# Turning the attended heads and their sums by VectorE block transposes in place of TensorE passes, in a four-layer gated cross-attention kernel

## What is computed

```python
query = _split_heads(q @ w_q.T + b_q)
key = _split_heads(k @ w_k.T + b_k)
value = _split_heads(v @ w_v.T + b_v)
scores = jnp.einsum('bhqd,bhkd->bhqk', query, key) / jnp.sqrt(jnp.asarray(D_K, query.dtype))
scores = jnp.where(mask == 0, jnp.asarray(-1000000000.0, scores.dtype), scores)
attn = jax.nn.softmax(scores, axis=-1)
out = jnp.einsum('bhqk,bhkd->bhqd', attn, value)
out = out.transpose(0, 2, 1, 3).reshape(B, -1, D_MODEL)
return out @ w_o.T + b_o
```

## Time and profile before

| | |
|---|---|
| median of 3 runs | 1608.25 us (1605.38 to 1609.08) |
| profiled execution, its own time | 1611.25 us |
| its span in the profile | 1609.4 us |
| PE busy | 1483.6 us, 92% |
| DVE busy | 1318.3 us, 82% |
| ACT busy | 1135.4 us, 71% |
| POOL busy | 1030.6 us, 64% |
| mean granted TensorE clock | 0.963 |

### The profile page before, as it was taken

One profiled execution on the slowest core, in us unless ns is written; L12 is line 12 of the kernel. 1 busy time (PEld: TensorE's weight loads), 2 busy tenths in 40 slices (PEclk: granted clock), 3 DMA queues, 4 the chain that ended last, 5 costly groups with the idle time before them and its releaser, 6 DMA issues.

```text
span 1609.4 us, 42630 instructions
## 1 busy us (share of the span) xinstructions
PE 1483.6 (92%) x14155; PEld 1141.0 (71%) x14155; DVE 1318.3 (82%) x3187; ACT 1135.4 (71%) x2057; POOL 1030.6 (64%) x1392
## 2 busy tenths in 40 slices
PE   3899999999999974478999999999999999999997
PEld 2788888888888863245676677777777777767666
DVE  4798888888888876787888889898988888898732
ACT  7798888888888743265666666676666666666664
POOL 4688888888888743324456565666656565665445
PEclk8899999999999995588999999999999999999999
DMA  6322322322322002422222232233322332233100
GB/s 225 107 73 67 96 67 65 97 65 74 89 65 72 1 1 85 139 83 72 78 81 75 83 88 79 79 87 85 87 81 78 84 86 78 82 83 86 56 17 21
DMA packets 197690, 125.45 MB, mean 78 GB/s; under 512 B 44400, under 2 KB 196848, under 8 KB 197360
## 3 DMA queue, kind: packets, MB, share of 16 engines
q1 hardware_dynamic: 197616, 124.48, 26.7%
HBM read 92.69 MB, written 25.17 MB: 73 GB/s over the span
## 4 chain that ended last, share of the span: by engine, by line
PE 46%; SPq 6%; DMA 3%; DVE 2%; issue 2%; POOL 1%; ACT 1%; POOLq 0%
PE b_bank L1837 27%; PE b_bank L1912 6%; PE b_scoreT L1894 4%; PE b_score L1877 4%; PE b_bank L1845 2%; SPq L1293 2%; DMA b_nmT<-b_nm 1%; SPq L1282 1%; PE b_bank L1989 1%; SPq L1309 1%; PE b_bank L1927 1%; DMA b_yT<-b_y 1%; SPq L1318 1%; DVE b_nm L1653 1%; SPq L1326 1%
## 5 line engine op out<-in xcount | busy, mean ns | idle before, releaser
L1471 ACT ACTIVATE b_E<-b_scoreT 128x1024 f32<-128x1024 f32 x256 | 262.2, 1024 | 151.4 <-PE b_scoreT L1894 151.1
L1653 DVE TENSOR_REDUCE b_nm<-b_score 128x4 bf16<-128x1024 f32 x256 | 313.3, 1224 | 57.4 <-PE b_score L1877 51.2
L31 ACT ACT_TABLE_LOAD x157 | 201.4, 1283 | 18.6 <-PEq L1059 15.2
L1837 PE MATMUL b_bank<-f,b_YT 128*128 128x256 bf16 x1536 | 193.0, 277 | 4.7 <-POOL b_YT L1404 4.6
L890 PE MATMUL bank<-hT,W1T 128*128 128x256 bf16 x1536 | 183.3, 273 | 2.4 <-DVE hT L706 1.6
L1837 PE MATMUL b_bank<-b_hT,f 128*128 128x256 bf16 x1536 | 183.4, 273 | 0.8 <-DVE X L1749 0.8
L890 PE MATMUL bank<-W2T,G 128*128 128x256 bf16 x1024 | 171.0, 272 | 6.7 <-DVE GT L780 6.2
L1837 PEld LDWEIGHTS b_bank<-f,b_YT 128*128 128x128 bf16 x1536 | 144.7, 99 | 40.8 <-issue 19.3
L1837 PEld LDWEIGHTS b_bank<-b_hT,f 128*128 128x128 bf16 x1536 | 147.7, 98 | 30.4 <-issue 12.6
L890 PEld LDWEIGHTS bank<-hT,W1T 128*128 128x128 bf16 x1536 | 147.9, 98 | 27.8 <-ACT G L549 4.1
L1388 POOL TENSOR_TENSOR b_v<-b_v,b_e 128x512 f32<-128x512 f32 x32 | 40.7, 1270 | 194.1 <-DVE b_e L1734 194.1
(11 more groups left out here) (222 smaller groups left out, 3537.1 us busy)
## 6 DMA issues: line engine op xcount, KB each, us to landing
b_Q<-q_dram SPq DMA_DIRECT2D x192, 64.0 KB, 2.5
b_K<-k_dram SPq DMA_DIRECT2D x192, 64.0 KB, 2.7
xin<-in_x SPq DMA_DIRECT2D x32, 256.0 KB, 3.1
ctxn<-in_ctx SPq DMA_DIRECT2D x32, 256.0 KB, 2.8
mask_in<-in_mask SPq DMA_DIRECT2D x32, 256.0 KB, 3.0
X<-in_x SPq DMA_DIRECT2D x32, 256.0 KB, 4.0
ctxt<-in_ctxT SPq DMA_DIRECT2D x32, 256.0 KB, 4.2
b_ctxt<-in_ctxT SPq DMA_DIRECT2D x32, 256.0 KB, 2.8
```

What stands on the lines that cost most here:

```text
L31: act.add_instruction(mybir.InstLoadActFuncSet(name=nc.get_next_instruction_name(), act_func_set_id=which, ins=[], outs=[]))
L1471: nc.scalar.activation(E[:, pair:pair + 2], scoreT_ps[:, :, :, :], ACT.Exp).then_inc(sig["E"], 1)
L1653: nc.vector.tensor_reduce(pair, score_ps[:, :, :, :], AX.X, ALU.max, negate=True).then_inc(sig["nm"], 1)
L1837: last = nc.tensor.matmul(out_tile, lhs(i, k), rhs(j, k), start=start and k == chunks[0] and (i, j) == TERMS[0], stop=stop and k == chunks ...
```

## The change

DVE's transpose turns each 32x32 block within its own place. With a head 32 rows high, one such instruction on a bank of 128x512 gives for each block of 32 tokens a square in which the tokens lie along the partitions, and the head's 16 values and its sum along the free axis. So the change makes the turn there, for all tokens together and straight from PSUM, and the turn back in the same way.

- ACT no longer has `heads_copy(0)` and `heads_copy(1)`.
- PE no longer has `heads_transposed(0)`, `(1)` and `attended_transposed`: 12 passes of 128x128 for each batch. The first part of `second_product` now stands ahead of the turn of `hn`.
- DVE gets `heads_turned(0)` behind `maxima(6)`, on batch a; `heads_turned(1)` behind `mlp_normalised`, on batch o; `inverse_sums` (one reciprocal of 32 elements on a partition) and `attended` (one product of 512) behind `scaled`; and `heads_back` (the turn back) behind `maxima(0)`. It loses two reciprocals of 16 and two products of 256.
- `attended_high` and `attended_low` read the result `oF` from SBUF, where they read a PSUM bank before.
- The order of features after the turn back differs from the one before; the output weights' rows and the values' bias are put in that order on the host (`by_heads`).
- Banks: OT0, OT1 and ON fall away. AV01 and AV23 now share bank 8 with hT, H1 goes to bank 9 with K and V, H3 to bank 7.

```diff
@@ TURNS
             7: [("xT", "xlo", L_QKV, 1, 1), ("Q", "qlo", L_QKV, 1, 1), ("FFN", "ob", L_FFN, 1, 1),
-                ("PROJ", "x3", L_PROJ, 1, 1), ("H0", "Y", L_MLP, 4, 1), ("V", "V", L_QKV, 1, 1)],
-            8: [("OT0", "on", L_PROJ, 2, 1), ("hT", "hlo", L_MLP, 1, 1), ("ON", "onlo", L_PROJ, 1, 1),
-                ("AV01", "oS", L_ATT, 2, 1), ("H1", "Y", L_MLP, 4, 2)],
-            9: [("OT1", "on", L_PROJ, 2, 2), ("K", "klo", L_QKV, 1, 1), ("AV23", "oS", L_ATT, 2, 2),
-                ("H3", "Y", L_MLP, 4, 4)],
+                ("PROJ", "x3", L_PROJ, 1, 1), ("H0", "Y", L_MLP, 4, 1), ("H3", "Y", L_MLP, 4, 4)],
+            8: [("hT", "hlo", L_MLP, 1, 1), ("AV01", "at", L_ATT, 2, 1), ("AV23", "at", L_ATT, 2, 2)],
+            9: [("K", "klo", L_QKV, 1, 1), ("H1", "Y", L_MLP, 4, 2), ("V", "V", L_QKV, 1, 1)],
@@ ACT
-                    act.wait_ge(sig["onT_mm"], done(o))
+                    act.wait_ge(sig["oF"], done(o))
...
-                    nc.scalar.activation(oT[:, 0], whole_bank(BANK["ON"]), ACT.Copy).then_inc(sig["onhi"], 1)
-
-                def heads_copy(g):
...
+                    nc.scalar.activation(oT[:, 0], oF[:, :, :], ACT.Copy).then_inc(sig["onhi"], 1)
@@ DVE
-                def attended(t):
...
+                def heads_turned(c, b):
+
+                    dve.wait_ge(sig["av_mm"], done(b, per=NH // HG, part=2 * c + 2))
+                    nc.vector.transpose(at[:, 2 * c:2 * c + 2].rearrange("p g b r -> p (g b r)"),
+                                        flat_bank(BANK[("AV01", "AV23")[c]])).then_inc(sig["at"], 1)
+
+                def inverse_sums():
+                    dve.wait_ge(sig["at"], done(o, per=C))
+                    nc.vector.reciprocal(rsum[:, :, :], at[:, :, :, DK]).then_inc(sig["rsum"], 1)
+
+                def attended():
+                    dve.wait_ge(sig["rsum"], done(o))
+                    nc.vector.tensor_tensor(on[:, :, :, :].rearrange("p b g d -> p g b d"), at[:, :, :, 0:DK],
+                                            rsum[:, :, :].rearrange("p g (b u) -> p g b u", u=1).to_broadcast(
+                                                [P, NH // HG, Q32, DK]), ALU.mult).then_inc(sig["on"], 1)
+
+                def heads_back():
+
+                    dve.wait_ge(sig["on"], done(o))
+                    if (due := done(o, back=1)) is not None:
+                        dve.wait_ge(sig["onhi"], due)
+                    nc.vector.transpose(oF[:, :, :].rearrange("p c s -> p (c s)"),
+                                        on[:, :, :, :].rearrange("p b (c e) d -> p c b (e d)", e=2)).then_inc(sig["oF"], 1)
...
-                    nc.vector.tensor_tensor(oT[:, 1], whole_bank(BANK["ON"]), oT[:, 0], ALU.subtract).then_inc(sig["onlo"], 1)
+                    nc.vector.tensor_tensor(oT[:, 1], oF[:, :, :], oT[:, 0], ALU.subtract).then_inc(sig["onlo"], 1)
...
                 if h:
                     mlp_normalised()
+                if o:
+                    heads_turned(1, o)
                 if n:
                     scaled()
                 if o:
-                    attended(0)
+                    inverse_sums()
+                    attended()
                 if m:
                     maxima(0)
+                if o:
+                    heads_back()
                 if q:
                     normalised_low()
...
-                if o:
-                    attended(1)
                 if m:
                     maxima(1)
...
                     maxima(6)
+                if a:
+                    heads_turned(0, a)
                 if w:
                     result()
@@ PE
-                if o:
-                    heads_transposed(0)
                 if m:
                     scores(0)
-                if o:
-                    heads_transposed(1)
                 if q:
                     normalised_transposed()
+                if w:
+                    second_product(0, 0)
                 if h:
                     mlp_transposed()
-                if w:
-                    second_product(0, 0)
...
-                if o:
-                    attended_transposed()
```

More of the change, by code:

```diff
@@ L1161, in phase_b @@
         E = sb("E", [P, RING, T, S], F32)
-        oS = sb("oS", [P, NH // HG, S], F32)
-        rsum = sb("rsum", [P, T, NH], F32)
-        on = sb("on", [P, T, D], F32)
+        Q32 = S // ONE
+        at = sb("at", [P, NH // HG, Q32, ONE], F32)
+        rsum = sb("rsum", [P, NH // HG, Q32], F32)
+        on = sb("on", [P, Q32, NH // HG, DK], F32)
+        oF = sb("oF", [P, C, S], F32)
         oT = sb("oT", [P, 2, C, S], BF16)
@@ L1556, in iteration @@
                     exponential(6)
-                    heads_copy(0)
                     exponential(7)
@@ L1562, in iteration @@
                     silu(1)
-                if a:
-                    heads_copy(1)
                 if h:
@@ L1982, in values_in @@
                     row_projection("V", 2, cT, "V_mm")
[L1984 to L1995, removed]
                 def output_projection():
@@ L2100, in col, with by_heads @@
         return np.ascontiguousarray(np.reshape(inputs[name], (-1, P)).T)
+    def by_heads(rows):
+        grid = np.reshape(rows, (2, 2, 4, DK, -1))
+        return np.ascontiguousarray(np.reshape(np.transpose(grid, (0, 2, 1, 3, 4)), (NH * DK, -1)))
     arrays = {
@@ L2112 @@
         "wqT": transposed("L1_xattn_w_q"), "wkT": transposed("L1_xattn_w_k"),
-        "wvT": transposed("L1_xattn_w_v"), "woT": transposed("L1_xattn_w_o"),
-        "b_q_col": col("L1_xattn_b_q"), "b_k_col": col("L1_xattn_b_k"), "b_v_col": col("L1_xattn_b_v"),
+        "wvT": transposed("L1_xattn_w_v"), "woT": by_heads(transposed("L1_xattn_w_o")),
+        "b_q_col": col("L1_xattn_b_q"), "b_k_col": col("L1_xattn_b_k"), "b_v_col": np.ascontiguousarray(np.reshape(by_heads(inputs["L1_xattn_b_v"]), (-1, P)).T),
         "b_o": row("L1_xattn_b_o"),
```

## The result

The changed kernel took 1665.88 us (1664.57 to 1672.65) against 1608.46 us (1605.38 to 1609.08) before: a ratio of 1.0365, interval 1.0345 to 1.0384. It is slower by 57 us, where 19 were forecast: the direction is right, the size is outside the range of 1608 to 1648.

A forecast was written before the change was run, and what follows sets the result against it. PE bound the kernel, with a ring through DVE 0.77 us behind that would take over. Late iterations 3.5, middle 18.2, end -3 gave +18.7 us on 1611.25, so 1630, less 3.0 for the median: 1627, range 1608 to 1648.

The forecast's parts named there:

- The step that failed: On PE, before `scores(1)` and `queries`: with 1.52 us less to do, it idles about 2.5 us an iteration.
- The ring: PE, ACT, POOL, DVE up to `normalised_low`, then PE from `queries`: only 0.77 us shorter than PE's own work before the change.
- +0.96 an iteration: Whole iteration: `queries` late by 1.45 us, 0.49 back where `attended_transposed` stood, so 28.75 us.
- How often: Over the batches: 7 iterations at 0.5 us, 19 at 0.96, 3 at the end winning 1 us each; +18.7 us.
- The end, where PE was to win: After the last `v`, with `v` and `cT` gone: PE is the bound again, 1 us won in each of 3 iterations.
- `heads_turned(0)` hidden: On DVE behind `maxima(6)`: its 0.60 us fall in the wait for `rs2`, cutting 1.02 us before `xh` to about 0.4.
- `heads_back` wasn't held: Rival on DVE behind `maxima(0)`: POOL holds `heads_back`, 0.79 us more in each iteration, 1645 us; chance 0.15.
- the 1.22 of two cycles an element: Rival on DVE's transposes: each needs two cycles an element, 1.22 us, giving 1657 us; chance 0.10.
- `v` was held: Forecast on DVE: POOL's `cT` holds `v` to 1.66 us from 1.03; the rival, not held, about 1610 us, chance 0.10.
- PE left the bound: Forecast at `queries`; the rival had PE stay the bound and the change win 34 us, 1575 us, chance 0.07.
- The prediction's estimate of 0.71 us for a transpose: On DVE, 512 elements at 0.96 GHz and one element a cycle; using it adds 0.06 us an iteration.

The follow-up runs named there:

- 16 matmuls: The changed kernel plus 16 matmuls that nobody reads, on PE where it waits for `maxima(0)` ahead of `scores(1)`: 1634.04 us, 1.0161 to the kernel before.
- eight matmuls: The changed kernel plus 8 idle matmuls on PE ahead of `scores(1)`: 1639.77 us, 1.0207 to the kernel before.
- all four moved: The changed kernel with `heads_turned(1)` behind `maxima(7)`, `inverse_sums` and `attended` behind `normalised_low`, `heads_back` behind `maxima(1)`: 1598.22 us, 0.9949 to the kernel before.
- one turn moved: The changed kernel with only `heads_turned(1)` moved, behind `maxima(7)` where DVE waits for `rs2`: 1636.29 us, 1.0176 to the kernel before.
- the filled run with `v` first: The changed kernel with `scaled` ahead of `heads_turned(1)` on DVE and 10 idle matmuls on PE ahead of `scores(1)`: 1618.97 us, 1.0087 to the kernel before.

## Why the direction was right and the size wrong

- **The step that failed:** "PE, with 1.52 us less to do, idles for about 2.5 us of it, in front of `scores(1)` and of `queries`". The idle time was found there and as long; it was counted as time in which PE does nothing, and as that alone. What it does to PE's clock afterwards was no term and no rival, though its signs stood in the trace of the kernel before. The runs put it at 1.5 us in 16 of 18 iterations, 32 us of the 57 (1665.88 against 1634.04). With the clock held the time would have been within the range. In the earlier trace rows, which the prediction read for `v` and for PE's wait alone, PE's turn of `hn` takes 1.06 us behind an idle 1.87, where the same turn takes 0.66 in the iteration of 1200 us. A window of the kernel before (columns as in the earlier trace rows) has the granted clock at 0.50 from there on:

```profile
759.70:763.10 3.40, 3.40 (x16) 2.39 (x16) 2.19 (x4) 0.60 (x1) 3.23 (x4) 0.50 0.47 101
```

- **The ring** was right. From the start of `xh` to the end of `normalised_low` it took 6.00 us before and takes 1217.96 - 1209.63 = 8.33 now; forecast were 8.19, and the 0.14 are those of `attended`.
- **+0.96 an iteration** was measured, with the clock held, as 29.08 - 27.82 = 1.26. About half of the 0.3 is `attended`; another 0.12 is the step from the end of `normalised_low` to the start of `queries`, 1218.11 - 1217.96 = 0.15 where the prediction allowed 0.03. The few hundredths left weren't followed up.
- **How often:** with 16 matmuls the 18 middle iterations give +22.7 us (18.2 forecast for 19) and the nine before them +1.5 (3.5 for seven). Near the end the clock fell in that execution too (0.50 from 1549.5 to 1556.3 us); with eight matmuls it stayed at 1.00 there, and the next three iterations give +0.2 (-3 forecast). That makes 24, where the sum said 18.7. The end, where PE was to win, didn't win.
- **`heads_turned(0)` hidden:** right, but in another place. The earlier trace rows show the same 1.02 us before `xh` as now. The wait that covers most of its 0.62 us lies earlier: `result`, behind it, waited 0.41 us for PE before and no longer does. DVE's timeline before, then after:

```profile
1203.00 0.75 DVE L1670 SCALAR_TENSOR_TENSOR b_res<-b_bank,half_gate,X 128x512 f32<-128x512 f32 x1 [0.41 <-PE b_bank L1837]
```

```profile
1205.17 0.71 DVE L1660 SCALAR_TENSOR_TENSOR b_res<-b_bank,half_gate,X 128x512 f32<-128x512 f32 x1
```

- **Rivals.** `heads_back` wasn't held (0.69 beside POOL's 0.61 and 1.16), the transposes took 0.70 us and not the 1.22 of two cycles an element, `v` was held, and PE left the bound. The Trainium skill's page "SBUF — State Buffer", section "SBUF: two separate sides", has a Vector instruction with two SBUF inputs and a POOL instruction that reads SBUF exclude each other, the one that starts first going through. The traces agree: `attended` took 0.83 us here, 0.99 in the run with all four moved and 1.35 with one turn moved, and POOL's additions 1.90 beside it here; where it began 0.01 us ahead of them, in the filled run with `v` first, it took 0.69 and they 1.95. `heads_back`, with one source, kept to 0.69 beside POOL. The prediction's estimate of 0.71 us for a transpose, from the Trainium skill's page "VectorE: DVE Perf Modes", section "The three transpose paths", stands beside 0.70 measured.

## What to carry to other kernels

When a change takes work from an engine at the bound and leaves it idle, ask of TensorE not only how long it idles but what its clock does next: here a gap of 1.9 us and one of 0.6 cost another 1.5 in most iterations, and 16 useless matmuls in the gap won back 32 us. Work moved to another engine belongs where that engine waits already; with four instructions on the ring from `rs2` to `queries` the change loses 57 us, with the same four beside it it wins 10. Look for the ring first, then for the place.

## What the runs showed of the hardware

- TensorE's granted clock fell to 0.51 for some 3 us after 1.87 and 0.58 us of idling, in 16 of 18 iterations; after 1.15 and 0.58 it fell in 10 of 18, and after 1.94 in one piece, in the kernel before, in 8 of 18, with waits that look alike in the trace. Where the fall sets in moves against the iterations, from one to the next; what sets it isn't shown.
- A DVE transpose of 128x512 in fp32 takes 0.70 us from PSUM or from SBUF, whether POOL ran beside it or not, while a product of the same size from two SBUF operands took 0.68 to 1.35 by when it met POOL.
